# Half of the last block's out-projection computed in the last scan steps, and four buffers for the last block's x2 rows

## What is computed

```python
x = x + mamba(cond(x, subjects))          # cond: a 64x64 matrix per subject along the sequence axis
# mamba: xz = h @ in_proj.T; x, z = split(xz)           (1024 channels each)
#        xc = silu(causal_conv4(x)); dt, B, C = split(xc @ x_proj.T)      (128, 16, 16)
#        delta = softplus(dt @ dt_proj.T + bias)
#        s_t = s_(t-1) * exp(delta_t * A) + delta_t * xc_t * B_t;  y_t = sum over 16 states of C_t * s_t
#        y = (y + xc * D) * silu(z);  return y @ out_proj.T              (1024 -> 512)
x = x + ffn(h @ W.T + lora(h))            # h is the x of the line above
# ffn: 16 experts, the best 4 of the best 2 of 4 groups, plus one shared expert
```

## Time and profile before

| | |
|---|---|
| three runs | 1980.17, 1984.63, 1985.88 us; median 1984.63 |
| the profiled execution | 1985.24 us, its span 1983.4 us |
| `mamba` | span 0 to 1233 us |
| of it, the list `AFTER` | from the last sum at 1154.4 to 1233 |
| `shared`, `experts` | 1233 us to the end |

### The profile page before, as it was taken

How to read it: one execution, slowest core, us unless ns; L and a number is a source line. 1 busy time by engine, 2 the same in 40 slices (tenths; PEclk the granted TensorE clock), 3 DMA queues, 4 the chain that set the end, 5 groups by cost and what they waited for, 6 DMA issues and landing times. The chain is left out here.

```text
span 1983.4 us, 28450 instructions
## 1 busy us (share of the span) xinstructions
PE 1705.8 (86%) x7908; PEld 1244.8 (63%) x7908; DVE 1490.2 (75%) x1992; ACT 801.4 (40%) x1188; POOL 1041.4 (53%) x813
## 2 busy tenths in 40 slices
PE   7768776898887987987867888899979999999998
PEld 4354434554445654554544555787869999899997
DVE  2699999999999999989999931758635656656564
ACT  2566566465564665573644511000012323323322
POOL 0287589694597875795967651000023434334333
PEclk9879897889996998986977878999989999999999
DMA  4112112222123232131221343111226566565664
GB/s 121 41 48 75 45 49 70 64 77 88 59 71 90 75 90 64 60 119 36 75 68 54 108 162 105 32 64 64 88 54 176 121 165 167 131 166 124 166 166 74
DMA packets 129895, 182.19 MB, mean 92 GB/s; under 512 B 21379, under 2 KB 79491, under 8 KB 126660
## 3 DMA queue, kind: packets, MB, share of 16 engines
q1 hardware_dynamic: 109540, 131.85, 20.5%
q0 software_dynamic: 17760, 44.05, 11.3%
q10 hardware_dynamic: 2432, 4.33, 0.8%
HBM read 276.45 MB, written 37.36 MB: 158 GB/s over the span
## 5 line engine op out<-in xcount | busy, mean ns | idle before, releaser
L1054 POOL TENSOR_TENSOR arena_kept<-arena_kept,b_all 128x512 f32<-128x512 f32 x512 | 636.7, 1272 | 338.7 <-DVE arena_kept L948 220.8
L948 DVE TENSOR_TENSOR_SCAN arena_kept<-da,arena_kept 128x512 f32<-128x512 f32 x512 | 599.4, 1210 | 34.2 <-ACT da L817 13.4
L613 PE MATMUL hT<-ident_kept,arena_kept 128*128 128x128 f32 x2048 | 328.5, 309 | 180.4 <-DVE yacc L961 112.9
L817 ACT ACTIVATE da<-arena_kept,a_neg 128x504 f32<-128x504 f32 x512 | 345.6, 684 | 316.5 <-DVE arena_kept L948 311.3
L613 PEld LDWEIGHTS hT<-ident_kept,arena_kept 128*128 128x128 f32 x2048 | 265.9, 159 | 293.5 <-DVE arena_kept L948 227.1
L961 DVE SCALAR_TENSOR_TENSOR yacc<-hT,c_now,yacc 128x512 f32<-128x512 f32 x480 | 334.8, 739 | 20.7 <-PE hT L613 19.6
L1942 POOL DMA_INDIRECT out<-y,slots_kept x76 | 135.2, 1778 | 256.7 <-issue 190.4
L463 PE MATMUL bank<-hid,wt 128*128 128x512 f32 x512 | 255.0, 647 | 6.4 <-ACT conv_sum L666 5.5
L463 PEld LDWEIGHTS bank<-hid,wt 128*128 128x128 f32 x512 | 102.7, 210 | 119.9 <-issue 110.5
L1578 POOL DMA_DIRECT2D slots_kept<-lists_kept x1 | 0.6, 554 | 249.5 <-DVE lists_kept L1528 249.5
L524 PE MATMUL bank<-skip,wt 128*128 128x512 f32 x256 | 128.4, 652 | 2.5 <-DVE skip L897 2.5
(11 more groups left out here) (221 smaller groups left out, 3148.8 us busy)
## 6 DMA issues: line engine op xcount, KB each, us to landing
w_up_kept<-in_up_T SPq DMA_DIRECT2D x76, 1408.0 KB, 5.7
w_dn_kept<-in_dn_T SPq DMA_DIRECT2D x76, 768.0 KB, 8.4
b_all<-bt_scratch SPq DMA_DIRECT2D x128, 256.0 KB, 3.5
wt<-in_in_T SPq DMA_DIRECT2D x64, 256.0 KB, 3.0
wt<-in_out_T SPq DMA_DIRECT2D x32, 256.0 KB, 3.0
res<-in_x_pad SPq DMA_DIRECT2D x16, 256.0 KB, 4.8
x_scratch<-res SPq DMA_DIRECT2D x16, 256.0 KB, 2.0
wt<-in_w_T SPq DMA_DIRECT2D x16, 256.0 KB, 3.0
```

The costliest lines, as they stand in the source:

```text
L613: mm = nc.tensor.transpose(turned_in(j, m, t)[:, d * P:(d + 1) * P], h[:, m % RING, d, t * P:(t + 1) * P], ident[:])
L817: nc.scalar.activation(out[:, :, 1:], rows[:, :, 1:], ACT.Exp, scale=a_neg[:, d, n:n + 1]) \
L948: nc.vector.tensor_tensor_scan(h[:, n % RING, i, :], da[i % RING][:], dbx[:, i, :], 0.0, ALU.mult, ALU.add).then_inc(scan_done, 1)
L1054: nc.gpsimd.tensor_tensor(dbx[:, i, :], u[:, d, :], b_all[:, m % RING, :], ALU.mult) \
```

## The change

- The four pieces `pre0` to `pre3` are put into steps 27 to 30 of the last body. Each is, for one feature tile, the first half's four matmuls of the out-projection and the residual's four (`pre_proj`); ACT copies the bank to `x1T`. The residual of the last block is therefore loaded at step 18 of the last body, not behind it.
- Behind the last step, `last_turn` adds xc*D on PE (one matmul 128x512 by the identity for each of the four banks) and turns `yacc` with accumulating matmuls, no longer with transposes; DVE does one multiplication for each (`gate_last`) in place of an addition and a multiplication. `post0` to `post3` are the second half's four matmuls each, and DVE adds them to `x1T` (`x1_rest`) where ACT copied before.
- The last block's four x2 row tiles go to four places (`x2_last`: the two of `x2_sb` and the two of `b_all`), so that the copies wait only for stores of the block before.
- POOL's split of the shared weights and DVE's split of x2 wait for the last `gate_last`.

```diff
-     ["ct", "dt1"], ["ln1", "dt2", "w2"], ["ln2", "z5", "w3"], ["dt3", "z6", "row0"],
-     ["ln3", "z7", "row1"], ["row2", "row3", "zsilu1"], ["lg"], []],
+     ["ct", "dt1"], ["ln1", "dt2", "w2"], ["ln2", "z5", "w3"], ["dt3", "z6", "row0", "pre0"],
+     ["ln3", "z7", "row1", "pre1"], ["row2", "row3", "zsilu1", "pre2"], ["lg", "pre3"], []],
...
-AFTER = ["turn1"] + [f"out{i}" for i in range(2 * KM)] + ["xa"] + [
+AFTER = ["turn1"] + [f"post{f}" for f in range(KM)] + ["xa"] + [
...
+    x2_last = [x2_sb[:, 0, :], x2_sb[:, 1, :], b_all[:, 0, :], b_all[:, 1, :]]
...
+                    if j == NBLK - 1 and m == step_of(f"xr{TB - 1}") + 4:
+                        load_res(NBLK)
...
-            load_res(NBLK)
+            for m in (STEPS, STEPS + 1):
+                for n in tiles_due(NBLK - 1, m):
+                    load_tile(n)
...
+            def last_turn(at):
+                pe.wait_ge(skip_ready, NBLK * DT + SKIP0)
+                for d in range(HT):
+                    bank = take(at, d)
+                    nc.tensor.matmul(bank[:], ident[:], skip[:, HT + d, :], start=True, stop=False)
+                    pe.wait_ge(sum_done, sums(NBLK - 1, STEPS - 1, TB - 1))
+                    for t in range(TB):
+                        mm = nc.tensor.matmul(bank[:, t * P:(t + 1) * P], yacc[:, t, d * P:(d + 1) * P], ident[:],
+                                              start=False, stop=(t == TB - 1))
+                    mm.then_inc(bank_full, 1)
...
+            def pre_proj(section, j, at, f):
+                bank = take(at)
+                pe.wait_ge(y_ready[0], (at.block + 1) * HT + Y0)
+                w = tile_of(section, j, f"pre{f}")
+                for d in range(HT):
+                    nc.tensor.matmul(bank[:], w[:, d, :], skip[:, d, :], start=(d == 0), stop=False)
+                pe.wait_ge(res_full, 16 * TB * NBLK)
+                for t in range(TB):
+                    mm = nc.tensor.matmul(bank[:, t * P:(t + 1) * P], res[:, t, f * P:(f + 1) * P], ident[:],
+                                          start=False, stop=(t == TB - 1))
+                mm.then_inc(bank_full, 1)
+
+            def post_proj(section, j, at, f):
+                bank = take(at)
+                w = tile_of(section, j, f"post{f}")
+                for d in range(HT):
+                    pe.wait_ge(dve_emptied, Place(section, j, "turn1").dve + d + 1)
+                    mm = nc.tensor.matmul(bank[:], w[:, d, :], skip[:, HT + d, :], start=(d == 0), stop=(d == HT - 1))
+                mm.then_inc(bank_full, 1)
...
-                act.wait_ge(x2_stored[t % RING], 16 * (TB // RING * (at.block - 1) + t // RING))
-                nc.scalar.copy(x2_sb[:, t % RING, :], banks[at.bank][:]).then_inc(act_emptied, 1)
+                if at.block < NBLK:
+                    act.wait_ge(x2_stored[t % RING], 16 * (TB // RING * (at.block - 1) + t // RING))
+                    nc.scalar.copy(x2_sb[:, t % RING, :], banks[at.bank][:]).then_inc(act_emptied, 1)
+                else:
+                    act.wait_ge(x2_stored[t % RING], 16 * TB // RING * (NBLK - 1))
+                    act.wait_ge(dbx_made, NBLK * SCANS + DBX0)
+                    nc.scalar.copy(x2_last[t], banks[at.bank][:]).then_inc(act_emptied, 1)
...
+            def gate_last(at, i):
+                d = HT + i
+                if i == 0:
+                    dve.wait_ge(zs_ready, NBLK * HALVES)
+                dve.wait_ge(bank_full, at.full + i + 1)
+                nc.vector.tensor_tensor(skip[:, d, :], banks[at.uses[i].bank][:], zs[:, d, :], ALU.mult).then_inc(dve_emptied, 1)
+
+            def x1_rest(at, f):
+                dve.wait_ge(bank_full, at.full + 1)
+                dve.wait_ge(act_emptied, Place("body", NBLK - 1, f"pre{f}").act + 1)
+                nc.vector.tensor_tensor(x1T[:, f, :], banks[at.bank][:], x1T[:, f, :], ALU.add).then_inc(dve_emptied, 1)
```

More of the change, by code:

```diff
@@ L71, in name_and_number @@
     return name, int(piece[len(name):] or 0)
-EMPTIED_BY_ACT = {"cond", "x", "rank", "bc", "dt", "z", "out", "xr", "w", "row", "lg"}
-EMPTIED_BY_DVE = {"turn", "ct", "xa"}
+EMPTIED_BY_ACT = {"cond", "x", "rank", "bc", "dt", "z", "out", "pre", "xr", "w", "row", "lg"}
+EMPTIED_BY_DVE = {"turn", "ct", "post", "xa"}
 EMPTIED = EMPTIED_BY_ACT | EMPTIED_BY_DVE
@@ L89, in runs @@
     name, i = name_and_number(piece)
+    if name == "pre":
+        return j == NBLK - 1
     if j == 0 and (piece == "turn1" or name in OF_LAST_BLOCK):
@@ L171, in turned_bc @@
     return Place("ahead", 0, "ct") if block == 0 else Place("body", block - 1, "ct")
-STREAMED = {"x", "z", "out", "xa", "w"}
+STREAMED = {"x", "z", "out", "pre", "post", "xa", "w"}
 STREAM = [(section, j, piece) for section, j, pieces in SECTIONS for piece in pieces
@@ L348, in load_tile @@
                     tile = out_wT[:, i % 2 * HT:i % 2 * HT + HT, i // 2 * P:(i // 2 + 1) * P]
+                elif name in ("pre", "post"):
+                    tile = out_wT[:, (HT if name == "post" else 0):(DT if name == "post" else HT), i * P:(i + 1) * P]
                 elif name == "xa":
@@ L372, in store_x2 @@
                 sp.wait_ge(act_emptied, Place(section, j, f"row{t}").act + 1)
-                sp.dma_start(x2_rows[j - 1, t], x2_sb[:, t % RING, :]).then_inc(x2_stored[t % RING], 16)
+                rows = x2_last[t] if j == NBLK else x2_sb[:, t % RING, :]
+                sp.dma_start(x2_rows[j - 1, t], rows).then_inc(x2_stored[t % RING], 16)
             sp.dma_start(itok_row[:], itok[0:BATCH].rearrange("b o -> o b")).then_inc(itok_in, 16)
@@ L531, in out_proj, with x1_made @@
                     mm.then_inc(bank_full, 1)
+            def pre_proj(section, j, at, f):
[16 more added lines that the diff above has]
+                mm.then_inc(bank_full, 1)
+            def x1_made(section, j):
+                if section == "after":
+                    pe.wait_ge(dve_emptied, Place(section, j, f"post{KM - 1}").dve + 1)
+                else:
+                    pe.wait_ge(act_emptied, Place(section, j, f"out{2 * KM - 1}").act + 1)
             def x1_row(section, j, at, t):
                 bank = take(at)
-                pe.wait_ge(act_emptied, Place(section, j, f"out{2 * KM - 1}").act + 1)
+                x1_made(section, j)
                 for k in range(KM):
@@ L588, in piece_of @@
                     dt_proj(section, j, at, i)
+                elif name == "turn" and section == "after":
+                    last_turn(at)
                 elif name == "turn":
@@ L592, in piece_of @@
                     out_proj(section, j, at, i)
+                elif name == "pre":
+                    pre_proj(section, j, at, i)
+                elif name == "post":
+                    post_proj(section, j, at, i)
                 elif name == "xr":
@@ L797, in piece_of @@
                     x1_out(at, i // 2)
+                elif name == "pre":
+                    x1_out(at, i)
                 elif name == "xr":
@@ L920, in split_first_x2 @@
                 dve.wait_ge(y_ready[0], NBLK * HT + Y0)
-                dve.wait_ge(y_ready[1], NBLK * HT)
+                dve.wait_ge(dve_emptied, Place("after", NBLK, "turn1").dve + HT)
                 hi_part(nc.vector, x2_hi, x2T_in).then_inc(first_upper, 1)
@@ L937, in piece_of @@
                     masked(at)
+                elif name == "post":
+                    x1_rest(at, i)
             def scan(j, g, n, i):
@@ L1010, in _ @@
             for i in range(HT):
-                add_skip(Place("after", NBLK, "turn1"), 1, i)
+                gate_last(Place("after", NBLK, "turn1"), i)
             for piece in AFTER:
@@ L1082, in _ @@
             pool.wait_ge(skip_ready, NBLK * DT + SKIP0)
-            pool.wait_ge(y_ready[1], NBLK * HT)
+            pool.wait_ge(dve_emptied, Place("after", NBLK, "turn1").dve + HT)
             for i, (hi, lo) in enumerate(parts["shared"]):
```

## The result

| | before | changed |
|---|---|---|
| first chip, runs of each | 4 | 4 |
| median, us | 1982.66 | 1964.29 (1963.04 to 1965.30) |
| ratio, 95% interval | | 0.9907 (0.9893 to 0.9921) |
| profiled execution, span | 1983.4 | 1961.9 |
| second chip, 11 and 6 runs, median | 1982.54 | 1966.63 (1964.47 to 1970.27) |

What follows compares the result with a forecast made beforehand. Behind the last sum, one chain paced by PE bounds the kernel. Terms -18.0 - 0.8 + 5.7 - 3.75 - 1.65 = -18.5 from 1985.24 us give 1966.7, forecast median 1966, range 1957 to 1975.

Steps and rivals of the forecast that it cites:

- The path: Behind the last sum all is one chain paced by PE; work added ahead is free only while PE idles there.
- The out-projection, -18.0: From the first projection matmul to the adapters: 16 matmuls left, 16.1 us in place of 34.10, a gain of 18.0.
- the 1.5 us added for the clock: In the first out-projection matmuls: 1.5 of the 2.2 us lost before to a slow clock was expected to remain.
- The last turn, -0.8: From the last sum to the first projection matmul: 6.2 us in place of 7.06, a gain of 0.8.
- the factor of four of the Trainium skill's page: Rival in the last turn: transposes four times faster than the matmuls replacing them; +3.5 us, 1969.5, chance 0.02.
- The steps, +5.7: Steps 27 to 31: 17.3 us of added PE work only partly finds room; the last sum comes 5.7 us later.
- Its bet: In the last scan steps: PE, its gaps filled, holds 2.4 GHz, so logits take 4.64 us and not 6.85.
- The rows and the logits, -3.75 and -1.65: Last x2 rows: no store wait, 3.75 us gained; logits behind them 4.64 in place of 6.29, 1.65 gained.
- the stores now end well ahead of the logits: End of the part before `shared`: with four row buffers, the x2 row stores finish well before the logits; no size given.
- B late: Loads of B for steps 30 and 31: cost 0 expected; rival, two waits of 2.04 us, +4.1, 1970, chance 0.05.
- The slow clock in the last turn: Rival: PE idles under the last additions, its clock falls, slowing turn, first projections and logits; +8.5, 1974.5, chance 0.16.
- Slower than before: Rival: PE falls to 1.2 GHz in the last five steps despite full work; up to +39.35, 2005, chance 0.03.

Runs made afterwards that it cites:

- the late silu: Changed kernel with the second half's silu(z) moved from step 29 to step 30 in all blocks; 41.70 us from step 27 to the last sum, whole run 1964.2 us.
- the doubled and quartered pieces: Changed kernel with each first-half piece's four wide matmuls done twice, or only one of them done; 57.13 and 35.55 us from step 27 to the last sum.
- the best version: Changed kernel with w2, w3 in steps 24, 25, first-half pieces in 26 to 29, logits and silu(z) in 30; median 1956.79 us, ratio 0.9865 to the kernel before.
- the version with the old turn: Changed kernel with PE transposes and DVE's addition and multiplication again, each projection matmul waiting for its own tile; turn 4.36 us, projection 16.99 us.
- one matmul of four: Changed kernel with one wide matmul instead of four in each first-half piece; 35.55 us from step 27 to the last sum.
- the pieces packed: Changed kernel with w2, w3 in steps 24, 25, first-half pieces in 26 to 29, logits alone in 30; 118.13 us from the second half's first to last sum.

## Why the prediction was right, and where it was not

- **The path.** Right: everything behind the last sum is one chain, and the last steps had room for a part of the added work only. The sum of the terms, -18.5, stands beside -18.4 and -15.9 in the medians of two chips, and -17.6 in the stretches. That it lies so near is in part luck: the out-projection brought 1.4 more than counted, and the steps cost 2.0 more in the execution profiled first.
- **The out-projection, -18.0.** Measured -19.4. The mis-sized term is the 1.5 us added for the clock: the projections ran at 1.00 from the first in every version with the new turn. The rest is as counted: 13.9 for 16 matmuls and 0.83 for the hand-over.
- **The last turn, -0.8.** Measured -0.76 (6.30 for the 6.2 counted). The four accumulating matmuls of a bank took 1165.35 - 1164.46 = 0.89 us, twice the four transposes, so the row decided against the factor of four of the Trainium skill's page ("TensorE: Matmul & The Clock Gate", Terms).
- **The steps, +5.7.** 41.70 or 41.71 us from step 27 to the sum in four executions of kernels that are the same up to there and in the one with the late silu, so +6.0; 43.40, +7.7, in the execution profiled first. The ledger of PE work was right, and the doubled and quartered pieces show that PE alone bounds these steps. Its bet was not: "with the gaps filled it should hold 2.4 GHz". The gaps were filled, and the clock fell in the logits all the same. It cost 1.3 to 1.5 us in the transposes, and 1.7 more where it reached into `pre3`; what kept the sum near was that the logits took 4.06 and not 4.64, and that the last sum came 1.4 us behind PE's last transposes and not 2.1.
- **The rows and the logits, -3.75 and -1.65.** Measured -5.18 and -4.38 in two executions. The wait went as counted (idleness ahead of the logits 0.19, 3.87 before). The logits were faster by 2.2 in one and 0.7 in the other. The step that failed is "the stores now end well ahead of the logits": where the logits took 4.56 us or less the last store ended the part, at 7.0 in any case. In the changed kernel it landed 0.68 behind the copied logits, and PE idled 1.63 us ahead of `shared` where it had idled 0.89.
- **B late, and what its price rested on.** The cost of 0 was right: POOL waited 4 to 5 us for B in steps 29 to 31 of the changed kernel, and DVE never for POOL. But the earlier trace rows were misread. The 2.04 us wait names ACT's decay, not POOL; ACT's timeline of the kernel before shows what stood ahead of that decay, silu(z) between two table loads:

```profile
1059.79 1.28 ACT L680 ACT_TABLE_LOAD   x1
1061.08 1.91 ACT L680 ACTIVATE arena_kept<-arena_kept 128x2048 f32<-128x2048 f32 x1
1063.01 1.28 ACT L681 ACT_TABLE_LOAD   x1
1064.30 1.29 ACT L817 ACTIVATE da<-arena_kept,a_neg 128x504 f32<-128x504 f32 x2
```

  The late B ended at 1062.43 beside it and was hidden. That misread wait was the one worth removing: its sister in step 31 is part of the best version's gain.
- **The slow clock in the last turn** did not come in the changed kernel; it came in the version with the old turn, where PE idles between the banks, and cost the projections 2.3 us, the 2.2 that had been put on them. A part of the turn was slow too with one matmul of four (7.16) and with the pieces packed (6.69), in both of which PE had idled ahead of step 31's transposes (2.18 and 1.73 us).
- **Slower than before** would have needed a mean clock under 0.68 in the last steps; it was 0.90.

## What to carry to other kernels

Work that is moved off the end into steps bounded by another engine costs what exceeds the slack of the engine that does it: add up that engine's work over the steps at full clock, set it against the steps' time, and expect them to grow by what does not fit; here 17.3 us of work moved in, 11.3 found room, and the steps grew by 6.0. Where in a step it stands matters as much as how much it is: a piece ahead of the last tile that the bounding engine waits for makes it wait, and a step that is left light wastes what a crowded one lacks. When one wait is gone, look for the next one on the same engine before leaving, by the engine that the row names and its own timeline; a wait that cost nothing while another engine was late counts once that is mended.

## What was not expected of the hardware

TensorE's clock fell from 1.00 to 0.50 while it was busy without a gap. In the changed kernel it had 1.00 from before step 27, was busy for all of the stretch, and was at 0.50 from 1145.6 to 1152.4: it fell 3.0 us behind the start of 32 matmuls with 16 moving columns, before their end. The same 32 left it at 1.00 in the last body of the version with the logits in step 28, and not in the two bodies before. No rule comes out of these figures: with the same pieces over the two steps ahead, it fell 3.0 us behind their start in the changed kernel and 3.9 in the packed version.

Four fp32 matmuls of 128x128 that accumulate take 0.89 us at 2.4 GHz, four transposes of that size 0.44.
